# Reordering stores, output products and first-row transposes in a two-pass attention and feed-forward kernel

## The reference

```python
h = _layernorm(x, ln1_g, ln1_b)
x = _attention(h, h, sa_wq, sa_wk, sa_wv, sa_wo, sa_bo) + x
h = _layernorm(x, ln2_g, ln2_b)
x = _attention(h, cond_emb, ca_wq, ca_wk, ca_wv, ca_wo, ca_bo) + x
h = _layernorm(x, ln3_g, ln3_b)
p = h @ ff_w1 + ff_b1
a, gate = (p[..., :D_FF], p[..., D_FF:])
h = a * gelu(gate) @ ff_w2 + ff_b2
return h + x
```

## Time and profile before

| | us |
|---|---|
| median of 3 runs | 2880.1 (2879.93 to 2884.04) |
| the profiled execution, its own time | 2885.6 |
| its span, first to last instruction | 2883.8 |
| TensorE busy | 2827.1 (98%) |
| VectorE busy | 2269.3 (79%) |
| ScalarE busy | 1919.2 (67%) |
| GpSimd busy | 1463.2 (51%) |

### The profile page before, as it was taken

The page is one execution under the profiler, slowest core; times in us unless marked ns, Lnnn a source line. Parts: engine busy times, 40 slices in busy tenths (PEclk is TensorE's granted clock), DMA queues, the critical chain, the costliest instruction groups (busy, mean ns, idle before and its releaser), DMA issues.

```text
span 2883.8 us, 72587 instructions
## 1 busy us (share of the span) xinstructions
PE 2827.1 (98%) x25278; PEld 2522.1 (87%) x25278; DVE 2269.3 (79%) x3495; ACT 1919.2 (67%) x6041; POOL 1463.2 (51%) x1310
## 2 busy tenths in 40 slices
PE   8999999999999999999999999999999999999999
PEld 7888888888888888888888888888888889999999
DVE  7788888888888888888888888888888865555554
ACT  6677777777777777777777777777777754444443
POOL 5444444444444444755555555555555554554454
PEclk9999999999999999999999999999999999999999
DMA  6666666666666666666666766666666632222222
GB/s 156 144 161 158 161 159 160 160 153 152 150 151 156 145 157 148 170 163 171 171 168 168 172 165 161 160 157 160 161 161 163 156 99 82 82 73 79 85 73 63
DMA packets 355329, 413.33 MB, mean 143 GB/s; under 512 B 122016, under 2 KB 209440, under 8 KB 355232
## 3 DMA queue, kind: packets, MB, share of 16 engines
q1 hardware_dynamic: 345088, 395.29, 56.6%
q10 hardware_dynamic: 10144, 16.78, 1.6%
HBM read 94.52 MB, written 49.02 MB: 50 GB/s over the span
## 4 chain that ended last, share of the span: by engine, by line
PE 56%; issue 17%; POOL 11%; DVE 8%; DMA 3%; ACT 2%; SPq 1%; POOLq 0%; DVEq 0%; ACTq 0%
PE unit_ps L612 30%; PE s_ps L612 12%; POOL probs L1322 9%; PE unit_ps L637 7%; PE s_ps L625 7%; DVE neg_max L1076 3%; DMA rows_t_dram<-row_blocks 2%; DVE blocks L1090 2%; POOL x_rb L1309 1%; SPq L529 1%; ACT probs L885 1%; DVE qk_lo L1101 1%; DMA rows_in<-rows_t_dram 1%; DVE hT_lo L1114 1%; POOL rstd L1301 1%
## 5 line engine op out<-in xcount | busy, mean ns | idle before, releaser
L1322 POOL TENSOR_TENSOR probs<-probs,row_inv 128x1024 f32<-128x1024 f32 x512 | 970.3, 1895 | 1103.4 <-DVE row_inv L1081 1103.3
L885 ACT ACTIVATE probs<-s_ps,neg_max 128x256 f32<-128x256 f32 x2048 | 950.6, 488 | 424.5 <-DVE neg_max L1076 424.5
L1090 DVE STREAM_TRANSPOSE blocks<-probs 128x1024 f32<-128x1024 f32 x512 | 632.8, 1236 | 94.7 <-POOL probs L1322 94.5
L1076 DVE TENSOR_REDUCE neg_max<-s_ps 128x4 f32<-128x1024 f32 x512 | 611.7, 1195 | 2.4 <-PE s_ps L625 2.4
L612 PE MATMUL unit_ps<-hT_hi,w_hi 128*128 128x256 f32 x2048 | 574.1, 283 | 0.7 <-DVE hT_lo L1114 0.7
L612 PE MATMUL unit_ps<-hT_hi,w_lo 128*128 128x256 f32 x2048 | 558.0, 278 | 0.0
L612 PE MATMUL unit_ps<-hT_lo,w_hi 128*128 128x256 f32 x1792 | 499.6, 279 | 0.0
L637 PE MATMUL unit_ps<-pT,v_f 128*64 128x256 f32 x4096 | 458.3, 381 | 3.5 <-issue 3.5
L1101 DVE TENSOR_TENSOR qk_lo<-unit_ps,qk_hi 128x512 fp32r<-128x512 f32 x512 | 347.2, 679 | 141.6 <-ACT qk_hi L917 133.3
L885 ACT ACTIVATION_READ_ACCUMULATOR probs<-s_ps,neg_max 128x1 f32 x2048 | 446.3, 218 | 0.0
L612 PE MATMUL unit_ps<-w_hi,a_hi 128*128 128x256 f32 x1536 | 433.8, 282 | 1.9 <-POOL a_lo L1337 1.0
(11 more groups left out here) (73 smaller groups left out, 6009.7 us busy)
## 6 DMA issues: line engine op xcount, KB each, us to landing
pT<-blocks SPq DMA_DIRECT2D x1024, 256.0 KB, 4.5
rows_t_dram<-row_blocks SPq DMA_DIRECT2D x91, 256.0 KB, 5.8
rows_in<-rows_t_dram SPq DMA_DIRECT2D x91, 256.0 KB, 2.9
x_res<-in_x_dram SPq DMA_DIRECT2D x32, 256.0 KB, 6.3
x_sa_dram<-x_out SPq DMA_DIRECT2D x32, 256.0 KB, 4.6
x_ln<-x_sa_dram ACTq DMA_DIRECT2D x32, 256.0 KB, 6.0
ctx_in<-in_ctx_dram SPq DMA_DIRECT2D x32, 256.0 KB, 4.7
x_res<-x_sa_dram SPq DMA_DIRECT2D x32, 256.0 KB, 6.7
```

The lines of the kernel that those rows point to most:

```text
L885: op = nc.scalar.activation(probs[:, m % 2, r, :].rearrange("p (j b c) -> p j b c", j=IT, c=BLK), scored.rearrange("p (j c b) -> p j b c", ...
L1076: nc.vector.tensor_reduce(neg_max[:, m % RING, :], s_ps[:, m % 2, :, :].rearrange("p h (i j) -> p (h i) j", j=S), AX_X, ALU.max, negate=Tr ...
L1090: nc.vector.transpose(blocks[:, n % 2, :, m % 2, :].rearrange("p b (j r c) -> p r j b c", j=IT, c=BLK), probs[:, m % 2, :, :].rearrange("p ...
L1322: nc.gpsimd.tensor_tensor(probs[:, m % 2, :, :], probs[:, m % 2, :, :], row_inv[:, m % RING, :].unsqueeze(2).broadcast_to([P, ROWS, S]), A ...
```

## The change

On SyncE, in step 3, the store of the transposed rows and the load of the residual go ahead of `move_blocks(t, 2)`. On ScalarE `scale_rows` goes behind the cast of qk5. On TensorE the old batch's output product (`wo1`) becomes the last unit of step 0's gap, and the second half of `wo0` the last of step 3's; banks 1 to 3 change hands for qk4, qk5 and wo1; the unit `x` of the first rows becomes the last of step 2, in bank 0. On VectorE the two `project_out` go behind the remainders of their step, qk2's remainder moves from the end of step 3 into the next step 0, `scale_inputs` goes to the end of step 2, and the scaling of the parameter tiles goes from the start of t = 1 to step 2 of t = 2. The waits at the end of attention follow the new banks.

```diff
--- before.py
+++ after.py
@@ -49,18 +49,18 @@
 
 
 STEP_UNITS = (
-    ((("qk", 3), "cur"), (("wo", 1), "old"), (("qk", 4), "cur"), (("qk", 5), "cur")),
+    ((("qk", 3), "cur"), (("qk", 4), "cur"), (("qk", 5), "cur"), (("wo", 1), "old")),
     ((("a", 0), "prv"), (("a", 1), "prv"), (("a", 2), "prv"), (("a", 3), "prv")),
-    ((("v", 0, 0), "cur"), (("qk", 6), "cur"), (("x",), "nxt"), (("qk", 7), "cur"), (("v", 0, 1), "cur"),
-     (("v", 1, 0), "cur"), (("v", 1, 1), "cur")),
+    ((("v", 0, 0), "cur"), (("qk", 6), "cur"), (("qk", 7), "cur"), (("v", 0, 1), "cur"), (("v", 1, 0), "cur"),
+     (("v", 1, 1), "cur"), (("x",), "nxt")),
     ((("wo", 0), "prv"), (("qk", 0), "nxt"), (("qk", 1), "nxt"), (("qk", 2), "nxt")),
 )
 ORDER = [user for step in STEP_UNITS for user in step]
 
 
-BANK_OF = {("qk", 3): 0, ("wo", 1): 3, ("qk", 4): 1, ("qk", 5): 2,
+BANK_OF = {("qk", 3): 0, ("qk", 4): 3, ("qk", 5): 1, ("wo", 1): 2,
            ("a", 0): 0, ("a", 1): 3, ("a", 2): 1, ("a", 3): 2,
-           ("v", 0, 0): 0, ("qk", 6): 3, ("x",): 2, ("qk", 7): 1, ("v", 0, 1): 0, ("v", 1, 0): 2, ("v", 1, 1): 3,
+           ("v", 0, 0): 0, ("qk", 6): 3, ("qk", 7): 1, ("v", 0, 1): 0, ("v", 1, 0): 2, ("v", 1, 1): 3, ("x",): 0,
            ("wo", 0): 1, ("qk", 0): 0, ("qk", 1): 3, ("qk", 2): 2}
 assert set(BANK_OF) == {u for u, _ in ORDER} and len(STEP_UNITS) == STEPS
 LAST_ATTENDED = (0, 3, 0, 3)
@@ -544,6 +544,12 @@
                 for n in range(STEPS):
                     if n == 0 and blocks_next(t, parts):
                         load_rows_transposed(at, t + 1, WHOLE)
+                    if n == 3 and blocks_ahead(t, parts):
+                        store_row_blocks(at, t + 2, WHOLE)
+                    if n == 3 and "cur" in parts:
+                        ph = pass_of(t, home)
+                        at_least(sp, at.xrb_done, t)
+                        sp.dma_start(x_res[:], tiles(ph.x_in[t - ph.first])).then_inc(at.res_ld, 16)
                     if n and "cur" in parts:
                         move_blocks(t, n - 1, home)
                     elif n == 0 and "prv" in parts:
@@ -562,12 +568,6 @@
                         load_output_weight(sa if t == 0 else ca, 0 if t == 0 else 1)
                     if n == 0 and isinstance(t, int) and t == 1:
                         load_output_weight(sa, 1)
-                    if n == 3 and blocks_ahead(t, parts):
-                        store_row_blocks(at, t + 2, WHOLE)
-                    if n == 3 and "cur" in parts:
-                        ph = pass_of(t, home)
-                        at_least(sp, at.xrb_done, t)
-                        sp.dma_start(x_res[:], tiles(ph.x_in[t - ph.first])).then_inc(at.res_ld, 16)
                     if n == 2 and parts == LAST:
                         load_rows(1, tiles(x_ca[1]))
 
@@ -737,9 +737,8 @@
             def end_attention():
 
                 last = TOTAL - 1
-                pe.wait_ge(at.v_done, 4 * last + 3)
+                pe.wait_ge(at.wo_done, 2 * last)
                 transpose_rows(0)
-                pe.wait_ge(at.wo_done, 2 * last - 1)
                 for it in range(IT):
                     project_out(last, 0, it, ca)
                 attend(last, 2, ca)
@@ -759,7 +758,7 @@
                     project_out(t - 1, 1, it, ca)
                 pe.wait_ge(at.v_done, 4 * t + 2)
                 attend(t, 0, ca)
-                pe.wait_ge(at.wo_done, 2 * t)
+                pe.wait_ge(at.v_done, 4 * t + 4)
                 attend(t, 1, ca)
 
             def attention_iteration(t, parts, home):
@@ -776,8 +775,8 @@
                         project_out(t - 1, 0, 0, home)
                         run_unit(t, home, ("qk", 0), "nxt")
                         run_unit(t, home, ("qk", 1), "nxt")
+                        run_unit(t, home, ("qk", 2), "nxt")
                         project_out(t - 1, 0, 1, home)
-                        run_unit(t, home, ("qk", 2), "nxt")
                     else:
                         for unit, part in units:
                             run_unit(t, home, unit, part)
@@ -996,9 +995,9 @@
                                 split_rows(t + 1, False)
                             if to_context:
                                 split_context(t + 1)
+                        split_unit(t, *user)
                         if user[0] == ("qk", 5) and blocks_next(t, parts):
                             scale_rows(t + 1, home)
-                        split_unit(t, *user)
                         if user[0] == ("qk", 7) and in_context and "nxt" in parts:
                             split_rows(t + 1, True)
                     if parts not in (SECOND, STEADY):
@@ -1153,6 +1152,11 @@
                 for k in range(DK):
                     op = scale_shift(ff, k, unit_ps[:, TURNED, k * S:(k + 1) * S])
                 op.then_inc(ff.h_done, 1)
+
+            def scale_context_norm():
+                dve.wait_ge(param_ld, PARAMS)
+                for a in (ln_gain, ln_bias):
+                    nc.vector.tensor_scalar(a[:, ca.norm, :], a[:, ca.norm, :], SCALE, None, ALU.mult).then_inc(rows_scaled, 1)
 
             def end_attention():
                 last = TOTAL - 1
@@ -1181,11 +1185,6 @@
                 if parts == DRAIN:
                     end_attention()
                     return
-                if isinstance(t, int) and t == 1:
-                    dve.wait_ge(param_ld, PARAMS)
-
-                    for a in (ln_gain, ln_bias):
-                        nc.vector.tensor_scalar(a[:, ca.norm, :], a[:, ca.norm, :], SCALE, None, ALU.mult).then_inc(rows_scaled, 1)
                 in_context = parts != FILL and pass_of(t, home).has_ctx
                 to_context = "nxt" in parts and pass_of(t + 1, home).has_ctx
                 for n in range(STEPS):
@@ -1209,10 +1208,8 @@
                         invert_sums(t, 2 * n)
                     if n == 2 and "prv" in parts:
                         attended_lo(t - 1, 3)
-                    if n == 2 and "nxt" in parts and by_tensor(t + 1):
-                        if parts == FILL:
-                            dve.wait_ge(norm_ld, 16 * 2)
-                        scale_inputs(t + 1, home)
+                    if n == 0 and "prv" in parts:
+                        qk_remainders(t, 2)
                     for pair in pairs[:{0: 2 if parts == START else 1, 1: 0, 2: 1, 3: 2}[n]]:
                         qk_remainders(*pair)
                     for sems, ph, b, s, _ in norms(t, parts, home):
@@ -1226,8 +1223,6 @@
                     for sems, ph, b, _, m in norms(t, parts, home):
                         if n == m:
                             norm_moments(sems)
-                    if n == 0 and "old" in parts:
-                        project_out(t - 2, 1)
                     if n != 1 and "cur" in parts:
                         transpose_blocks(t, 2 * n, home)
                     if "cur" in parts:
@@ -1237,12 +1232,20 @@
                         attended_lo(t - 1, 2)
                     if n == 1 and "cur" in parts:
                         transpose_blocks(t, 2 * n, home)
+                    for pair in pairs[{0: 2 if parts == START else 1, 1: 0, 2: 1, 3: 3}[n]:]:
+                        qk_remainders(*pair)
+                    if n == 0 and "old" in parts:
+                        project_out(t - 2, 1)
                     if n == 3 and "prv" in parts:
                         project_out(t - 1, 0)
-                    for pair in pairs[{0: 2 if parts == START else 1, 1: 0, 2: 1, 3: 2}[n]:]:
-                        qk_remainders(*pair)
+                    if n == 2 and "nxt" in parts and by_tensor(t + 1):
+                        if parts == FILL:
+                            dve.wait_ge(norm_ld, 16 * 2)
+                        scale_inputs(t + 1, home)
                     if n == 2 and blocks_ahead(t, parts):
                         transpose_rows(at, t + 2)
+                    if n == 2 and isinstance(t, int) and t == 2:
+                        scale_context_norm()
                     if n == 2 and "nxt" in parts and in_context:
                         x_remainder(t + 1)
                     if parts == FILL:
```

## The result

| | before | changed |
|---|---|---|
| median, us | 2882.07 (2879.93 to 2884.17, 4 runs) | 2836.99 (2836.61 to 2837.26, 4 runs) |
| ratio to before, 95% | | 0.9842 [0.983, 0.9854] |
| profiled execution: span | 2883.8 | 2834.8 |

The change makes the kernel faster by 1.6%, 45.1 us between the medians. The first view to read is again the windows, in the stretches of the earlier trace rows (columns as there).

The account below looks back on a forecast made before the run. TensorE bounds the self pass; late rows from DRAM, through ScalarE and VectorE, stall it in the cross pass. Cross 42.6, turn 2.9, reserve -4.6, start 2.5: 43.4 us off, and 5.5 from profile to median, forecast 2837 us (2828 to 2855).

Parts of the forecast that it names:

- SyncE and ScalarE: Cross pass: earlier store and load, qk5's cast ahead of scaling, remove the late-rows chain, priced at 1.47 us an iteration.
- about 6 us before ScalarE asks: Step 0: load of the rows goes out at its start, so rows are there that early.
- within step 3: SyncE: the store goes out some 7 us earlier, so its 6.3 us to landing end in that step.
- VectorE, step 0: 1.89 us wait goes, wo1's sum costs 0.6; step about 1.3 us shorter, 1.9 an iteration with step 3.
- A margin of only 0.4 to 0.5 us: Cross pass: VectorE saves 1.9 us an iteration against 1.47 that TensorE can give, so TensorE's list sets the time.
- the first rival: VectorE stays the bound in the cross pass; an iteration gains only 0.5 to 0.9 us, about 2856; chance 0.14.
- The slower rival: wo1's wait decides in both passes, 0.85 us in each of 61 iterations; about 2888 us; chance 0.05.
- wo1's wait: TensorE, step 0: wo1 in bank 2 waits for qk2's remainder, fits by 0.3 us; 0.15 us an iteration taken.
- the reserve of 0.15: Allowance per iteration for wo1's wait and other near misses, ends 0 and 0.5; 31 x 0.15 = -4.6 us.
- the 34.40 of t = 63: Last cross iteration before the change, without rows to scale: 34.40 us against 35.87, the basis for 1.47 an iteration.
- Self pass: Same edits, TensorE has no idle time to give back: price 0, ends -1 and +6.
- First rows: Start: small scaling moved -1.5, x last about -2 at t = 1 and +1 at t = 0; sum -2.5, ends -5 and +1.

Follow-up runs that it names:

- the hybrid: Changed kernel with step 0's old TensorE order and banks, wo1's sum and qk2's remainder where VectorE waits for GpSimd, x in its old place; 2833.73 us, 0.9837.
- x back, qk2's remainder too: Changed kernel with unit x back between qk6 and qk7, scale_inputs back, and qk2's remainder in step 3 ahead of wo0's sum; 2840.03 us, 0.9843.
- x back: Changed kernel with unit x back between qk6 and qk7 in bank 2 and scale_inputs ahead of qk6's remainder; 2836.81 us, 0.9835.

## Why the prediction was right, and where by luck

**SyncE and ScalarE: right.** Iterations 34.49 us (forecast 34.4 to 34.6), the `hT` and `v_f` waits gone, lag 1.06 (1.0 to 1.3). That the two edits are alternatives, not terms, I had half said: "even rows that came late would now hold only the exponentials". One figure was wrong. The rows were to be there "about 6 us before ScalarE asks"; they are there 2.7 us before. Two steps failed. The 6 us are how much earlier the load goes out, and of these 1.74 us only make up for the wait that was there, so some 4.6 were left. And the load was to take what it took before; it now stands directly behind the block move and takes 2.1 us longer (2.9 to 5.0). The landing of the store "within step 3" came true with room to spare, in 2.5 us and not 6.3.

**VectorE, step 0: right, and the margin was real.** "A margin of only 0.4 to 0.5 us" was tested by putting 0.6 us back where they count (qk2's remainder in step 3): the iteration grew by 0.17 and the lag of step 1 by 0.74 us. By an estimate from these numbers, half a microsecond more on top would have brought the first rival; no run went there. The slower rival had no ground: wo1's wait came to 0.23 us an iteration, not 0.85.

**wo1's wait: mis-sized, 0.15 against 0.23.** The remainder was to fit by 0.3 us. It nearly does. TensorE around wo1 in the iteration shown above:

```profile
1490.64 0.28 PE L612 MATMUL unit_ps<-hT_hi,w_lo 128*128 128x256 f32 x1
1490.79 0.38 PE L612 MATMUL unit_ps<-w_hi,a_hi 128*128 128x256 f32 x1
1491.01 0.28 PE L612 MATMUL unit_ps<-w_lo,a_hi 128*128 128x256 f32 x1
```

The remainder of qk2 is the first of the pair at 1490.00 and ends between 1490.6 and 1490.7. The starts around wo1's first matmul are 0.15 and 0.22 us apart instead of 0.11, so 0.15 us are lost here although no wait is listed. In the kernel with qk2's remainder in step 3 the same two intervals are 0.113 and 0.115 us (medians of 28 iterations), and in the changed kernel 0.145 and 0.220, so it is this release and not the change of product that costs. TensorE reaches the place 5.5 us after the step began, as worked out; what I left out is that a semaphore released just in time costs as much as a short wait. The changed kernel gets 0.14 us of it back by what the next point describes, which leaves 0.09 us of the reserve of 0.15 used: 34.49 us against the 34.40 of t = 63.

**Self pass: 5.1 us gained where 0 was forecast.** "TensorE has no idle time to give back" was true, and "price 0" did not follow; the gain lies outside the ends that the term had. The step that failed is the silent one, that a matmul costs the same wherever it stands. The kernel before, self pass, the first matmul of wo1, the first and the last of the two units behind it; then the changed kernel, the first of the same two units, and the first and the last of wo1 behind them:

```profile
747.45 0.28 PE L612 MATMUL unit_ps<-w_hi,a_hi 128*128 128x256 f32 x1
...
750.17 0.28 PE L612 MATMUL unit_ps<-hT_hi,w_hi 128*128 128x256 f32 x1
...
752.88 0.28 PE L612 MATMUL unit_ps<-hT_hi,w_lo 128*128 128x256 f32 x1
```

```profile
744.46 0.28 PE L612 MATMUL unit_ps<-hT_hi,w_hi 128*128 128x256 f32 x1
...
747.18 0.28 PE L612 MATMUL unit_ps<-w_hi,a_hi 128*128 128x256 f32 x1
...
749.79 0.28 PE L612 MATMUL unit_ps<-w_hi,a_lo 128*128 128x256 f32 x1
```

wo1 has 24 matmuls, and so have qk4 and qk5 together. Before: wo1 2.72 us from its first start to the next block's, 24 intervals of 0.113; behind it 2.71 us over 23 intervals, 0.1178 each. Changed: 2.72 us over 24 and 2.61 over 23, 0.113 and 0.1135. So qk4 and qk5 ran at 0.118 us behind wo1 and run at 0.1135 ahead of it, and so it is with qk2 and the second half of wo0: 36 x 0.0043 = 0.15 us an iteration, and 29 x 0.15 = 4.4 of the 5.1 us; the rest is the one long iteration of the kernel before. The runs bear it out by parts: SyncE's edit alone leaves 36.24 us, the new order in step 3 alone (the hybrid) gives 36.19, both steps give 36.09, and the reordering without SyncE and ScalarE has its 8.69 and 8.64 us in steps 3 and 0. It would be easy to conclude that a product slows whatever follows it. Step 3 of the changed kernel says no. The second matmul of wo0's first half, then the first of qk0 right behind that half, then the first of qk2:

```profile
770.61 0.28 PE L612 MATMUL unit_ps<-w_lo,a_hi 128*128 128x256 f32 x1
...
771.90 0.28 PE L612 MATMUL unit_ps<-hT_hi,w_hi 128*128 128x256 f32 x1
...
774.63 0.28 PE L612 MATMUL unit_ps<-hT_hi,w_hi 128*128 128x256 f32 x1
```

Here the product itself, behind the scores, is the slow one, 1.29 us over 11 intervals or 0.117, and qk0 and qk1 behind it take 2.73 over 24, or 0.1138; it is so in the kernel before too. So there are two paces, a unit keeps the one it starts with but for its first intervals, and the order of the units decides which it gets. What in the order decides no run shows, and I leave it open.

**First rows: -2.5 forecast, -0.5 in the one profile.** That is within the ends of the term, but its parts were not as forecast. The one that failed is "at t = 0 x as the last unit brings its rows later by about 1 us". TensorE at t = 0, unit v10, before, and then changed, with GpSimd's part:

```profile
40.31 0.40 PE L612 MATMUL unit_ps<-w_hi,hT_lo 128*128 128x512 f32 x1
40.55 0.40 PE L612 MATMUL unit_ps<-w_lo,hT_hi 128*128 128x512 f32 x1
```

```profile
37.12 2.34 POOL L1320 TENSOR_TENSOR w_lo<-w_stage,w_hi 128x1024 fp32r<-128x1024 f32 x1 [1.28 <-ACT w_hi L832]
...
39.61 0.76 PE L612 MATMUL unit_ps<-w_hi,hT_hi 128*128 128x512 f32 x1 [3.17 <-POOL w_lo L1320]
40.17 0.63 PE L612 MATMUL unit_ps<-w_hi,hT_lo 128*128 128x512 f32 x1
40.60 0.63 PE L612 MATMUL unit_ps<-w_lo,hT_hi 128*128 128x512 f32 x1
```

The windows from 39.5 to 43 us, before and then changed (the clock is the number after the five engines):

```profile
39.50:43.00 3.50, 3.03 (x12) 2.18 (x12) 3.36 (x7) 2.68 (x10) 2.08 (x2) 1.00 0.90 232
```

```profile
39.50:43.00 3.50, 3.39 (x8) 2.75 (x9) 2.87 (x6) 2.60 (x10) 2.08 (x2) 0.50 0.90 218
```

With x at the end nothing fills TensorE's wait for the split of v's weights, 3.17 us, and behind it the granted clock is 0.50, the level of 1.2 GHz, where before it was 1.00: the matmuls start 0.43 us apart instead of 0.24. t = 1 begins 3.1 us later (35.9 us after the first scores instead of 32.7). Twelve matmuls at 0.2 us more each are 2.4 of that, by an estimate from these rows. The other kernels tell the place of x from the clock (idle time just before v10, its clock, and the times from the first scores to those of t = 1 and of step 3 of t = 2):

| kernel | x | idle, us | clock, 39.5 to 43 us | to t = 1 | to step 3 of t = 2 |
|---|---|---|---|---|---|
| before | old | 1.58 | 1.00 | 32.7 | 102.2 |
| x back, qk2's remainder too | old | 2.36 | 1.00 | 32.7 | 100.4 |
| x back | old | 2.35 | 0.52 | 33.4 | 101.4 |
| changed | last | 3.17 | 0.50 | 35.9 | 101.7 |
| changed, SyncE's edit undone | last | 3.18 | 0.63 | 34.7 | 100.5 |
| changed, small scaling back | last | 1.67 | 1.00 | 33.1 | 98.9 |

At the full clock x as the last unit costs 0.4 us at t = 0, and at the low one up to 3.1. The low clock came behind every wait of 3.17 us or more, behind 2.35 us in one kernel and not in another, and the last row waited less because TensorE had run at the lower level earlier, from 30.6 us on. So how long a start takes is in part luck: those with the same order of the first rows differ by up to 2.7 us, and a finer split than this is not to be had. What x gives at t = 1 pays for its price at t = 0 in the changed kernel (from the first scores of t = 1 to step 3 of t = 2, 3.6 us less than before). That with x in its old place the kernel takes the same time (2836.81 us) says that the two are about even.

**Why the number fits so well.** Two of my errors cancel. I took 43.4 us off the profiled execution and 5.5 more for its distance to the median; the profiled execution fell by 49.0 and now lies on its median (2834.8 + 1.8 = 2836.6). The gain was larger by 5.6: self pass 5.1, cross pass and turn 2.3 (the reserve of 0.15 an iteration was not used up), start 2.0 the other way, end 0.2. The 5.5, in turn, was no constant of the kernel: it was where one execution lay in a spread of 4.2 us. That the changed kernel's four runs lie within 0.65 us is no property of it either; its variants, run four or five times, spread over 1.9 to 4.4 us. So the mechanism in the cross pass was right, the gain was forecast at 43.4 us where the profiles show 49.0, and that the median was met so closely was luck.

## What to carry to other kernels

Where an engine waits for a transfer, ask first what stands behind the waiting instruction; moving that ahead of it was worth as much here as making the transfer quick, and where the wait remained, it cost nothing. A small store on the path goes ahead of a big move in the same queue, and its time to landing is that of its place, not of its size. Work that must go onto a nearly full engine belongs where it waits for another engine anyway, and an engine that is busy for 100% can still gain from the order of its own list.

## What the runs showed that I had not expected

- A matmul of 256 columns starts 0.1135 us after the last in some units and 0.118 in others, for 12 to 24 matmuls on end, and always the same in the same place of the order. The place decided, not the kind of unit: qk4 and qk5 went from 0.118 to 0.1135 when the product before them was moved behind them.
- A 256 KB store lands in 2.5 us ahead of a block move of 1 MB and in 6.4 behind it; the load the other way round, 2.9 and 5.0.
- After 3.17 us without work TensorE's granted clock was 0.50 for the next 3.5 us, in the start of the changed kernel; its variants show 0.50 to 0.63 behind waits of 3.17 to 3.19 us. At it a matmul of 512 columns takes 0.2 us more.
- Putting one cast ahead of a scaling that waited for a transfer made the wait itself nearly vanish in one kernel (1.9 us left of 42.3) and left 30.2 us of it in another, and both were as fast.
- An instruction of VectorE on two values per partition takes 0.13 us ahead of GpSimd's product and 0.88 and 1.50 beside it. The rule that I had weighed, in the Trainium skill on its page SBUF — State Buffer, section "SBUF: two separate sides", foretells that: it says that the instruction that starts first holds the shared ports to its end and the other waits, and it names the two kinds of VectorE instruction to which this happens, those in a mode that uses two ports and, against a GpSimd instruction that reads SBUF, those with two inputs there. The trace agrees: both slow ones end within 0.03 us of the product beside them, and the quick one gives the row for the other case. An instruction of the second kind shows it too: `hT_lo` takes 0.69 us in the self pass, where it does not meet `normalise`, and 1.40 in the cross pass of the kernel before, where it starts 1.04 us into one.
